# Cross-attention of a decoder layer: the exponentials of a step on ScalarE put in front of the copy of the former unit's output

## The reference

```python
q = (query @ wq).reshape(bs, sq, 32, 128).transpose((0, 2, 1, 3))
k, v = key @ wk, value @ wv                 # 8 heads, each repeated for 4 query heads
q, k = _apply_rope(q, 0), _apply_rope(k, 0)
raw = jnp.einsum('bhqd,bhkd->bhqk', q, k) / scale
attn = jax.nn.softmax(raw + mask, axis=-1)
out = jnp.einsum('bhqk,bhkd->bhqd', attn, v)
return out.transpose((0, 2, 1, 3)).reshape(bs, sq, 32 * 128) @ wo
```

## Time and profile before

| what | value |
|---|---|
| time, median of 3 runs | 875.88 us (873.24 to 876.21) |
| profiled execution, its own time | 875.86 us |
| its span | 874.1 us |
| mean granted TensorE clock | 0.991 |
| busy over the span | PE 97%, PEld 80%, DVE 77%, ACT 52%, POOL 65% |
| ACT L1165, the copy that is moved | x64, mean 599 ns, 38.3 us busy |
| ACT L1145, the exponentials | x256, mean 391 ns, 99.3 us busy |
| idle time of ACT in front of L1165 | 201.9 us, ended by PE |
| idle time of DVE in front of L1514 | 20.4 us, ended by ACT L1165 |

### The profile page before, as it was taken

One profiled execution on the slowest core, in us unless ns is written; L12 is line 12 of the kernel. 1 busy time (PEld: TensorE's weight loads), 2 busy tenths in 40 slices (PEclk: granted clock), 3 DMA queues, 4 the chain that ended last, 5 costly groups with the idle time before them and its releaser, 6 DMA issues.

```text
span 874.1 us, 15787 instructions
## 1 busy us (share of the span) xinstructions
PE 844.3 (97%) x4676; PEld 700.2 (80%) x4676; DVE 677.0 (77%) x2114; ACT 453.8 (52%) x1516; POOL 565.7 (65%) x538
## 2 busy tenths in 40 slices
PE   7999999999999897999999999999999999999996
PEld 6788888788877676888888888888888787778884
DVE  5466888888876998888898889888888967546646
ACT  4336988778752434454555555545554565440320
POOL 4625866766675676678787787878785877455002
PEclk9999999999999999999999999999999999999998
DMA  8679998967760211122222222122221331000001
GB/s 278 261 230 216 221 195 172 181 155 149 191 212 34 87 43 35 56 71 64 65 66 71 63 65 64 64 64 64 65 63 65 108 116 46 24 13 25 25 2 47
DMA packets 82581, 88.27 MB, mean 101 GB/s; under 512 B 8129, under 2 KB 61633, under 8 KB 82497
## 3 DMA queue, kind: packets, MB, share of 16 engines
q1 hardware_dynamic: 82496, 87.26, 37.1%
HBM read 64.13 MB, written 23.07 MB: 100 GB/s over the span
## 4 chain that ended last, share of the span: by engine, by line
PE 78%; DVE 11%; issue 5%; ACT 3%; POOL 1%; DMA 1%; POOLq 0%; DVEq 0%; ACTq 0%; SPq 0%
PE banks L35 62%; PE banks L1279 6%; PE banks L1262 3%; PE banks L752 2%; PE banks L770 1%; PE banks L743 1%; DVE C_t L1403 1%; DMA stage<-wv_dram 1%; ACT B_prob L681 1%; DVE B_prob L840 1%; DVE C_t L1398 1%; DVE C_t L1404 1%; PE banks L122 1%; PE banks L367 1%; POOL B_wv L171 1%
## 5 line engine op out<-in xcount | busy, mean ns | idle before, releaser
L35 PE MATMUL banks<-C_wo,C_o 128*128 128x512 f32 x768 | 192.2, 399 | 1.7 <-issue 1.2
L35 PEld LDWEIGHTS banks<-C_wo,C_o 128*128 128x128 f32 x768 | 139.6, 188 | 30.6 <-ACT C_o L1165 1.6
L1165 ACT ACTIVATE C_o<-banks 128x512 fp32r<-128x512 f32 x64 | 38.3, 599 | 201.9 <-PE banks L35 201.9
L1563 POOL TENSOR_TENSOR C_q<-C_t,C_t 128x512 f32<-128x512 f32 x64 | 84.7, 1324 | 52.8 <-DVE C_t L1404 52.2
L681 ACT ACTIVATE B_prob<-B_prob,B_top 128x128 f32<-128x128 f32 x256 | 99.6, 392 | 26.1 <-DVE B_top L840 26.1
L1145 ACT ACTIVATE C_prob<-C_prob,C_top 128x128 f32<-128x128 f32 x256 | 99.3, 391 | 16.4 <-DVE C_top L1491 15.7
L593 POOL TENSOR_TENSOR B_prob<-B_prob,B_rden 128x512 f32<-128x512 f32 x64 | 67.7, 1059 | 36.9 <-DVE B_rden L849 36.9
L1570 POOL TENSOR_TENSOR C_prob<-C_prob,C_rden 128x512 f32<-128x512 f32 x64 | 72.4, 1131 | 18.4 <-DVE C_rden L1501 18.4
L35 PE MATMUL banks<-xT,C_block 128*128 128x512 f32 x288 | 71.2, 389 | 0.0
L840 DVE CUSTOM_DVE_ANT_0 B_prob<-banks,causal 128x128 f32<-128x128 f32 x256 | 58.9, 286 | 14.5 <-issue 13.3
L1279 PE MATMUL banks<-C_kv,C_q 128*128 128x128 f32 x512 | 67.8, 275 | 1.4 <-DVE C_top L1491 1.4
(11 more groups left out here) (186 smaller groups left out, 2048.3 us busy)
## 6 DMA issues: line engine op xcount, KB each, us to landing
C_kv<-cross_kv_d SPq DMA_DIRECT2D x64, 192.0 KB, 2.3
cross_kv_d<-B_v_out SPq DMA_DIRECT2D x16, 512.0 KB, 4.0
stage<-wq_dram SPq DMA_DIRECT2D x32, 256.0 KB, 2.6
stage<-wo_dram SPq DMA_DIRECT2D x32, 256.0 KB, 2.6
heads_q<-heads_q_d SPq DMA_DIRECT2D x96, 64.0 KB, 3.8
heads_k<-heads_k_d SPq DMA_DIRECT2D x96, 64.0 KB, 3.8
heads_q_d<-cT SPq DMA_DIRECT2D x8, 512.0 KB, 2.9
heads_k_d<-cT SPq DMA_DIRECT2D x8, 512.0 KB, 2.9
```

Source lines behind the costliest of these rows:

```text
L35: mm = eng.matmul(out, stationary[i], moving[j], start=first and n == 0, stop=last and n == len(PASSES) - 1)
L1563: eng.tensor_tensor(self.query(r), by_batch(t1), by_batch(t2), ALU.add).then_inc(self.s_sum, 1)
```

## The change

In `AttendCross.scalar`, which issues ScalarE's work of a step, the exponentials of unit n (and the negation of the mask, which step 0 alone has) now come before the copy of the P·V result of unit n-2. The copies of weight pieces (`pieces_hi`) stay behind both. Nothing else is changed: the same instructions, waits and semaphores, in another order on this one engine. Step 1 has no exponentials here (they are issued in `scalar_turned` of step 2), steps 0 and 1 have no copy, and steps 64 and 65 have a copy and no exponentials.

```diff
         if n == 2:
             self.pieces_hi(eng, 1)
+        if n == 0:
+            self.negate_mask(eng)
+        if n != 1:
+            self.exponentials(eng, n)
         if self.live(n, 2):
             eng.wait_ge(self.s_pv, n - 1)
             wait(eng, self.s_y, n - 2)
             eng.activation(self.o[0][:, :], self.ov, ACT.Copy).then_inc(self.s_ohi, 1)
-        if n == 0:
-            self.negate_mask(eng)
         if n != 1:
-            self.exponentials(eng, n)
             self.pieces_hi(eng, n)
```

## The result

The changed kernel takes 918.86 us (median of 4 runs, 917.07 to 923.97) against 874.88 us (873.24 to 876.21) beside it: 1.0524 times as long, with a 95% interval of 1.0499 to 1.0550. The prediction was 923.9 us. The profiled execution of after took 917.07 us, its span is 915.3 us and its mean granted clock 0.991, the same as before. It is the quickest of the four, which took 917.07, 917.11, 920.61 and 923.97 us; the two longer ones have granted clocks of 0.987 and 0.988 and no trace.

A forecast was written before the change was run, and what follows sets the result against it. The prediction took VectorE to bound the start, TensorE the middle with VectorE close behind, the end mixed; the change passes the middle to VectorE's loop. 9 + 31 + 8 = +48 us on 875.9 gave 923.9 us, range 902 to 948.

The forecast's parts named there:

- The loop: Middle, steps 10 to 54: VectorE's closed loop through minima, exponentials and o copy sets the step, +31 us.
- The path of 2.29: Each reordered step: from the last minimum's read-out through exponentials and o copy to the start of VectorE's L1514, 2.29 us.
- 1.68 us in each step: Steps 2 to 63: VectorE must stand 1.68 us before L1514, against 0.96 us a step to spare in the middle.
- The term of C_h: Middle, the step kind rotating C_h from SBUF: VectorE-GpSimd collisions add 1.1 us to 7.40, bounds 0 to 2.2.
- The start: Cross-attention up to step 10: VectorE is already the limit and cannot take up the delay, together +9 us.
- 8.4 + 1.07: Start: 8.4 us for five steps, 2 to 6, and +1.07 for step 7, where VectorE waited for the o copy anyway.
- The end: Steps 55 to 63: +2.2, then +1.68 each in 56 and 57, 0 in 58 to 60, more from 61; together +8 us.
- +2.3 predicted: End, steps 61 to 63: the new path adds 1.3 us in step 61 and 0.5 each in 62 and 63.
- (a): Rival: in the middle VectorE's slack takes up the whole delay, only start and end count; 893 us, chance 0.08.
- (b): Rival: TensorE's clock falls to half behind the new stalls in the middle; 952 us, chance 0.10.
- (c): Rival: earlier exponentials remove TensorE's 7.8 us of idle time at the start; 868 us, chance 0.02.
- (d): Rival: nothing measurable, overlooked slack meets VectorE's wait at start and end too; 876 us, chance 0.03.

The follow-up runs named there:

- e7: Changed kernel with GpSimd's low halves of weight pieces (L171) cut from 512 columns to 32 in steps 12, 16 and so on to 48: 909.64 us against 874.4.
- e5: Kernel before with the new order in steps 0 to 9 only and the old order from step 10: 885.72 us against 874.4, 1.0136.
- e3: Kernel before with the o copy also waiting for the row minima, ahead of all four exponentials: 880.7 us against 873.3, 1.0090.
- e8: e3 with ScalarE's copy of the transposed weights (L1156) issued before the block copies in one phase: 876.49 us against 874.06, 1.0027.
- e1: Changed kernel with two of the four exponentials in front of the o copy and two behind it: 886.54 us against 873.3, 1.0153.
- e9: Changed kernel with VectorE's minima put ahead of the two sine parts of the rotation: 878.6 us against 874.06, 1.0045.
- e6: Changed kernel with VectorE's L1515 moved from the end of its step to behind the next step's cosine: 910.16 us against 874.4, 1.0407.

## Why the prediction was right, point by point

**The loop.** Predicted were steps of 8.08, 7.40, 7.40 and 8.50 us, 31.4 in four. From one L1515 to the next after has 7.98, 7.38, 7.38 and 8.46, or 31.2. Step 9's L1515 starts at 368.21 and step 54's at 718.89: 350.7 us where the sum had 353.3. The path of 2.29 (measured 2.28), VectorE's wait of 1.6 in each of the 45 steps and the o copy 1.66 behind the last minimum (measured 1.67) came as reckoned, from single steps of before. TensorE's wait came out as a sum of 18.9 us in 357.2, 0.41 a step and not 0.7, and it is not even. It waits 1.3 us in the eleven longest steps (14.2 of it), and little in the others. The other third of the 27.9 us stands as busy time: in the 350.3 us of the middle TensorE is busy for 331.3, where it was 322.4. Its products have not become longer: those with wo take 399 ns in both kernels, and all groups of the middle together sum to 367.5 us where they had 366.8. What has changed is how far the records of consecutive products overlap, and their ends are modelled; so this is waiting in gaps too short to be listed, which the groups of waits alone would have missed. That reading is argued and not tested. VectorE's wait for the transposed weights is gone from the waits; of before it was (353 to 682 us)

```profile
DVE C_pT L1507 <- ACT C_pT L1156: 21.3, 27, 1.1
DVE C_o L1514 <- ACT C_o L1165: 10.3, 23, 0.6
```

and these 31.6 us are part of the 71.8 of after. This is why 1.68 us in each step did not cost 1.68.

**The term of C_h.** Taken at 1.1 us over a plain step: measured 8.46 - 7.38 = 1.08. Its size was right and its make-up was not. I had the encounters at the sines, with GpSimd's normalisation over before the last of the three. That last one is indeed free (689 ns) and the first sine meets the normalisation (1054 ns), +0.36. But most of it, 0.9, is the cosine, which runs into the low half of a weight piece on GpSimd (L171, 1.30 us, at 391.94), and e7 showed it by shortening that. (The addition in front of the cosine gives 0.14 back: the cosine starts 0.59 behind it and not 0.73.) A term with the right sum and wrong parts is half luck. The bounds that I gave, 0 to 2.2, were what covered it.

**The start.** +10.4 measured, +9 predicted, and e5 gave +11.0 for it alone. Counted from the first scores, L1515 falls back by 1.65, 1.69, 1.41, 2.23, 1.70 and 2.64 us in steps 2 to 7, which is 11.3, where 8.4 + 1.07 was reckoned. TensorE's wait that was 1.19 at 317.40 was to become 2.9, and it is 2.86 to 2.97 in two steps and 1.86 between them:

```profile
309.01 4.57 PE L35 MATMUL banks<-xT,C_w 128*128 128x512 f32 x12 [2.97 <-DVE C_t L1405]
...
322.92 3.01 PE L35 MATMUL banks<-xT,C_w 128*128 128x512 f32 x12 [1.86 <-DVE C_t L1405]
...
336.30 4.58 PE L35 MATMUL banks<-xT,C_w 128*128 128x512 f32 x12 [2.86 <-DVE C_t L1405]
...
356.75 1.53 PE L35 MATMUL banks<-C_pT,C_kv 128*128 128x512 f32 x3 [4.27 <-issue]
```

What I had not foreseen is that the clock falls there, three times, for 3.3 us at 0.50. The table of windows, by the columns given above:

```profile
309.10:312.40 3.30, 3.30 (x8) 2.65 (x9) 3.30 (x4) 0.00 (x0) 3.22 (x3) 0.50 0.02 5
336.40:339.70 3.30, 3.30 (x8) 2.64 (x9) 2.84 (x4) 0.01 (x1) 3.30 (x3) 0.50 0.00 0
356.90:360.20 3.30, 3.30 (x8) 2.53 (x9) 1.71 (x8) 2.65 (x10) 3.09 (x5) 0.50 0.20 58
```

Each costs TensorE some 1.6 us of work. VectorE sets the pace there, but the falls reach it through the transposed weights: behind the first it waits for them 0.45 us at 314.69, and behind the second 2.74, where the like wait of before was 1.14 (at 333.18):

```profile
341.98 0.69 DVE L1508 TENSOR_TENSOR C_pT<-banks,C_pT 128x512 fp32r<-128x512 f32 x1 [2.74 <-ACT C_pT L1156]
```

So the two falls cost VectorE about 2 us by step 7, which the prediction had at nothing, and step 7 was mis-sized by them: +2.64 for +1.07. e5 bears this out. It has a fall more, ahead of its step 6, and waits 0.43 us for the transposed weights there, where after has no fall and no such wait; from L1518 of step 5 to that of step 6 e5 takes 13.93 us and after 13.37, which is the 0.6 between +11.0 and +10.4. That the whole start came out only 1.4 above the forecast is partly luck. Before had one fall there too, from 345.8 to 352.6 us, twice as long (rows 7 has its first half).

**The end.** +6.0, predicted +8. By steps, from one output product to the next, after against before: 55 to 56 is 7.37 for 5.16 (+2.2, as predicted), 56 to 57 7.37 for 5.71 (+1.66, predicted 1.68), and 57 to 58 6.91 for 6.25: +0.66, where 1.68 was predicted. That is the part of this term that was mis-sized. I had added the 1.68 to before's step there, as if VectorE's work between stayed what it was. In this C_h step it is less than in those of the middle:

```profile
733.64 0.69 DVE L1515 TENSOR_TENSOR C_o<-banks,C_o 128x512 fp32r<-128x512 f32 x1 [1.59 <-ACT C_o L1169]
734.25 0.68 DVE L1399 TENSOR_TENSOR C_t<-C_h,trig 128x512 f32<-128x512 f32 x1
...
740.55 0.69 DVE L1515 TENSOR_TENSOR C_o<-banks,C_o 128x512 fp32r<-128x512 f32 x1 [1.59 <-ACT C_o L1169]
```

The cosine takes 0.68 in place of 1.64 and comes 0.61 behind L1515 in place of 1.20, as an addition of block products between them (L1418) is no longer there; so the loop is 6.91 for 8.46. GpSimd's piece was over at 734.25 (L171 ran from 732.98 for 1.27), where in the middle two block sums in front of it had kept it until 393.24. From 61 on it was +0.86, +0.46, +0.53 and -0.4, for +2.3 predicted.

**The rest.** Outside cross-attention 3.0 us went the other way, where I had nothing. 1.6 of them are behind it, where before's profiled execution has a stretch at half clock from 782.7 and after's has none; 1.4 are ahead of it, where the kernels do not differ. The profiled executions of all kernels here fall in two kinds by that: 122.9 to 123.0 us behind cross-attention without the fall near its beginning, 124.5 to 124.7 with it, whatever the order in cross-attention; and the part ahead of it took 273.6 to 275.9 in them. So neither belongs to the change. Against the profiled executions the forecast has 6.7 us too much (48 for 41.3): these 3.0, 3.1 in the middle and 2.0 at the end, less 1.4 at the start. Against the medians it is 4 (48 for 44.0), since the execution with the trace was the quickest of its kernel.

**What I did not count.** Behind the moved copy's wait stands ScalarE's own queue, with the copy of the transposed weights at its end. e3 and e8 show this path to be worth 4.8 us in the middle when it stands alone. In the changed kernel it costs nothing: there the exponentials come first and start right at the minima as before, and VectorE is so late that L1508 finds its copy done. The prediction named who waits for the moved instruction, and forgot those that stand behind it on its own engine. That held here by cover and not by reasoning; e1, with two exponentials in front, has it showing again.

**The rivals.** TensorE stays the bound (a): fell, 27.9 us are in the middle, and VectorE's loop sets it. The Trainium skill (Perfetto Trace Analysis, Identifying the Most-Contended Engine) has the engine of the highest occupancy improved first; as the prediction took it, this would have left the middle alone. This case's trace does not agree: TensorE has the highest occupancy after the change too (338.3 of 357.2 us in the middle), and yet a reordering on ScalarE, busy 167 of 357, lengthened the kernel by 5.2%. The clock falls in the middle (b): fell, the granted clock there is 1.00, with waits of 1.3 us in every fourth step. It did come true at the start, and at a fraction of the price. What the Trainium skill describes (TensorE: Matmul & The Clock Gate, HAM oscillation), the clock coming down anew in each round of a loop, is seen in three steps of the start of after and four of e5's, and nowhere in the middle of either. Faster (c) and no change (d) fell with the result.

## What to carry to other kernels

When an instruction is moved behind a wait, follow who needs it until the path comes back to the engine that makes the wait end. If it does, the step is at least that engine's own work between the two points plus the path through the others, however much slack a single step shows; and neither engine need look full. The remedy is to have that engine do work in the gap which waits for nobody (e9: 40 of 44 us back by putting VectorE's minima ahead of its two sine parts), and not work that waits itself (e6). And count what stands behind the moved instruction on its own engine as well as who waits for it (e3: 7.4 us).

## What the runs showed of the hardware

The granted clock of TensorE fell to 0.50 behind waits of 2.97, 2.86 and 4.27 us, in each case for some 3.4 us, and did not fall behind one of 1.86 or behind those of 1.3 in the middle. I had expected nothing of the first two. The prediction had bounded this by the fall of before alone, one behind 3.26 us. Nor does the length of the wait decide by itself: in e5, whose first ten steps are those of after, the clock fell also behind waits of 1.87 and 1.85 us. The second of these, and the window in it, with columns as above:

```profile
338.64 4.58 PE L35 MATMUL banks<-xT,C_w 128*128 128x512 f32 x12 [1.85 <-DVE C_t L1408]
...
339.40:342.60 3.20, 3.20 (x9) 2.42 (x9) 2.19 (x3) 0.00 (x0) 3.20 (x4) 0.50 0.02 5
```

A multiplication of 128 x 512 on VectorE out of two tiles in SBUF took 1.64 us beside an operation of 1.30 us on GpSimd that had begun 0.20 before it, and 0.68 when that operation was cut to 32 columns; out of PSUM it took 0.69. The encounter cost 0.96 of the 1.10 us that the two overlapped. In the first sine (64 x 512) it was 0.36 of 0.51. It set the length of the kernel only where VectorE's loop set the step.
